# Two layer norms as tensor_scalar, and the router's exponentials as powers of e on GpSimd

## The chip, the cores and the metric

One core of one Trainium2 chip. The metric is the device time of one execution in microseconds. The engines are TensorE (PE in the views, PEld its weight load), VectorE (DVE), ScalarE (ACT), GpSimd (POOL) and SyncE (SP, which issues DMAs). Each engine works through its own queue in order; semaphores tie them together.

## What is computed

An attention block over 8x8 windows and a mixture of experts, on 8 images of 192 channels and 16x16 pixels (2048 tokens of 192 channels).

```python
x = x + attention(_ln_c(x), Wq, Wk, Wv, Wo_w, Wo_b, rel_pos_bias)   # 12 heads, windows of 64 tokens
t = _to_tokens(x)
t = t + ffn(_ln_t(t), Ws, bs, W1, b1, W2, b2)

def ffn(x):
    route_prob = softmax(xt @ Ws + bs)                # 9 experts
    p, routes = max(route_prob), argmax(route_prob)
    h = gelu(xt @ W1 + b1)                            # 192 -> 768
    out = h @ W2 + b2                                 # 768 -> 192
    final = where(routes == 0, common, p * sel + (1 - p) * common)

def _ln_t(v, eps=1e-05):
    return (v - mean(v)) / sqrt(var(v) + eps)         # over the 192 channels; _ln_c is the same with 1e-06
```

The softmax of the router needs, beside the place of the largest logit, only its probability p: one over the sum of the nine exponentials of (logit - largest logit).

## The kernel before

The 2048 tokens are 16 tiles of 128 tokens (a tile is [128, 192], tokens on the partitions). The program has two stages, and every engine has one list of instructions for both.

**Attention stage.** A software pipeline of steps. In step s each engine runs a fixed program of small functions, each on tile s minus its own lag (DVE_PROGRAM, POOL_PROGRAM and so on hold name and lag). The DVE order in a step is: statistics of the first norm (L862, L864), values (L886), transposed weights (L913), residual and statistics of the second norm (L930 to L935), xh (the second norm, L942), normed (the first norm, L856), head_blocks (L874, two instructions, ka and kc), add_bias (L895), normalise (L921, L925), row_max (L903), and in some steps pieces of the routing. POOL's order is: rstd_1 (L556, L558: variance plus eps, then to the power -1/2), softmax_shift (L550, 128x768, subtracts the row maxima), the low half of one piece of a first weight matrix (L579 and L586), rstd_2 (L556, L558), xh_low (L572), the low half of a piece of a second weight matrix (L591), and from step 12 a scatter of a finished tile's rows to DRAM (L597). In step 2 POOL also clears nine blocks of weights (L605).

Both norms read x2 (the tile), mv (mean and variance per token) and rstd (one over the deviation per token), and write a [128, 192] f32 tile: xn for the attention, xhf for the experts. PE transposes xn (L1108), ACT copies it out (L667), and PE makes queries, keys and values from it in the next step. ACT copies the queries (L674); head_blocks waits for that copy, the scores on PE wait for head_blocks, and so on.

**Expert stage.** 39 tiles: 13 tiles through the common expert 0, 23 tiles of tokens sorted by expert, and the last 3 common ones. PE computes hidden(n) (30 matmuls, L1630) and outputs(n-1) (19 matmuls, L1654 and L1659); ACT applies gelu twice to each half of hidden(n) (hp in f16 at L1429, hf in f32 at L1432); DVE subtracts to get the low part (L1543), and both parts are needed before outputs(n). Tiles 0 to 4 overlap with the end of the attention stage. At tile DRAIN = 5 DVE copies the shifted logits lg to ex (L1581) and works out from the counts which expert each of the 23 tiles has: tile_counts (L1485 to L1496) and, behind its low parts and keep_y, tile_experts (L1502 to L1515). ACT takes the exponential of ex (L1447, 128x144 f32) behind its gelus of tile 5. DVE's probabilities (L1473 to L1477) wait for it behind the low parts of tile 6 and give pmax and omp, which the outputs of all later tiles are scaled with.

POOL's list continues, behind the last scatter, with the addresses of the sorted tiles and the scatter of their outputs (L1372 to L1378).

Of the kernel before, what the change touches and what calls it, by code (L numbers as in the profile page):

```python
# [1 line left out]

# [3 lines left out]
F32 = mybir.dt.float32  # L6
# [3 lines left out]
ALU = mybir.AluOpType  # L10
ACT = mybir.ActivationFunctionType
# [3 lines left out]
B, C, IMG = 8, 192, 16  # L15
# [4 lines left out]
NT = B * IMG * IMG // T  # L20
TPI = IMG * IMG // T
CH = 96
NE, FF = 9, 768
# [25 lines left out]
DRAIN = 5  # L49
# [31 lines left out]
def build(nc, x, Wq, Wk, Wv, Wo_w, Wo_b, rpb, rel, Ws, bs, W1, b1, W2, b2, out):  # L81
# [4 lines left out]
    with ExitStack() as whole:  # L86
# [47 lines left out]

        stage_1 = attention(nc, locals())
        stage_2 = experts(nc, locals(), stage_1)
        fused(nc, stage_1, stage_2, whole)

# [44 lines left out]
def attention(nc, g):  # L183
# [17 lines left out]
    with ExitStack() as ctx:  # L201
        def sb(name, shape, dt):
            return ctx.enter_context(nc.sbuf_tensor(name, shape, dt))
# [4 lines left out]
        def sem(name):  # L208
            return g["whole"].enter_context(nc.semaphore(name))
# [3 lines left out]
        xn = sb("xn", [128, C], F32)  # L213
# [9 lines left out]
        xhf = sb("xhf", [128, C], F32)  # L223
# [9 lines left out]
        mv = sb("mv", [128, 2, 2, 2], F32)  # L233
        rstd = sb("rstd", [128, 2, 2], F32)
# [81 lines left out]
        xn_ready = sem("xn_ready")  # L316
# [26 lines left out]
        xh_ready = sem("xh_ready")  # L343
# [159 lines left out]
        def gpsimd_part(pool):  # L503
# [98 lines left out]
            def zero_rows(experts):  # L602

                for e in experts:
                    pool.memset(w1s[LC:128, e, BIAS, :], 0.0).then_inc(w1_zeroed, 1)  # L605
                pool.wait_ge(w1_zeroed, experts[-1] + 1)
# [169 lines left out]
        def vector_part(dve, tile):  # L776
# [75 lines left out]
            def normed(t):  # L852
                dve.wait_ge(rstd1, t + 1)
                if t >= 1:
                    dve.wait_ge(xnT_mm, t)
                dve.scalar_tensor_tensor(out=xn[:, :], in0=x2[:, t, :], scalar=mv[:, 0, t % 2, 0:1],  # L856
                                         in1=rstd[:, 0, t % 2:t % 2 + 1].to_broadcast([128, C]),
                                         op0=ALU.subtract, op1=ALU.mult).then_inc(xn_ready, 1)

            def statistics_1(t):  # L860
                dve.wait_ge(x_kept, t + 1)
# [75 lines left out]
            def xh(t):  # L937
                dve.wait_ge(rstd2, t + 1)
                if t >= 1:
                    dve.wait_ge(xh_hi, t)  # L940
                    dve.wait_ge(xh_lo, t)
                dve.scalar_tensor_tensor(out=xhf[:, :], in0=x2[:, t, :], scalar=mv[:, 1, t % 2, 0:1],  # L942
                                         in1=rstd[:, 1, t % 2:t % 2 + 1].to_broadcast([128, C]),
                                         op0=ALU.subtract, op1=ALU.mult).then_inc(xh_ready, 1)

            def keep_logits(t):
                dve.wait_ge(lg_mm, t + 1)
# [62 lines left out]
            table_low()  # L1010
            one_hots(0)
            normed(0)
            away_from_row(1)
            one_hots(1)
            more_constants()
            statistics_1(1)
            keep_values_1(0)
            head_blocks(0)
            normed(1)
            tails()  # L1020
            for step in range(2, STEPS):
                if step == 2:
                    small_weights()
                stages(step, DVE_PROGRAM, (statistics_1, normed, head_blocks, keep_values_1, add_bias, row_max,
                                           weightsT_1, normalise, residual, xh, keep_logits, choose, slots), None)
                if 0 <= step - DRAIN_STEP < DRAIN:
                    tile(step - DRAIN_STEP)
# [254 lines left out]
def experts(nc, g, front):  # L1282
# [21 lines left out]
    def routed_at(j):  # L1304
        return FIRST + j
# [5 lines left out]
    with ExitStack() as ctx:  # L1311
        def sb(name, shape, dt):
            return ctx.enter_context(nc.sbuf_tensor(name, shape, dt))

        def sem(name):
            return g["whole"].enter_context(nc.semaphore(name))
# [2 lines left out]
        hp = sb("hp", [128, 2, 2, NF, T], F16)  # L1319
        y0 = sb("y0", [128, DRAIN, C], F32)  # L1320
        ex = sb("ex", [128, NT, NE], F32)
        big = sb("big", [128, NE * NR], F32)
        cnt = sb("cnt", [128, 5, NE], F32)
        ejf = sb("ejf", [128, 5, NR], F32)
# [14 lines left out]

        chain = sem("chain")  # L1340
        ex_in = sem("ex_in")
        ex_out = sem("ex_out")
        count_mm = sem("count_mm")
        home_kept = sem("home_kept")
# [21 lines left out]
        out_stored = [sem(f"out_stored{i}") for i in range(OB)]  # L1366

        def gpsimd_part(pool):
            pool.wait_ge(front["rows_zeroed"], 16)
            for j in range(NR):  # L1370
                pool.wait_ge(id_loaded[j % YB], 16 * (j // YB + 1))
                pool.tensor_tensor(home_f[:, 1:2], tid[:, j % YB, 1:2], jint[:, j:j + 1], ALU.mult  # L1372
                                   ).then_inc(home_sums, 1)
                pool.wait_ge(home_sums, j + 1)
                pool.tensor_tensor(home[:, j:j + 1], tid[:, j % YB, 0:1], home_f[:, 1:2], ALU.add).then_inc(home_kept, 1)
                pool.wait_ge(home_kept, j + 1)
                pool.wait_ge(y_kept, routed_at(j) + 1)
                pool.indirect_dma_start(out=ys, out_offset=bass.IndirectOffsetOnAxis(ap=home[:, j:j + 1].bitcast(U32), axis=0),  # L1378
                                        in_=yo[:, j % YB, :], in_offset=None
                                        ).then_inc(y_stored[j % YB], 16)  # L1380
# [41 lines left out]
        def scalar_part(act):  # L1422
            def hidden(n):
                for h in range(2):
                    act.wait_ge(h_mm[h], n + 1)
                    if n >= 2:
                        act.wait_ge(h_lo[h], n - 1)
                        act.wait_ge(y_mm, n - 1)
                    act.activation(hp[:, n % 2, 0, HF * h:HF * h + HF, :],  # L1429
                                   p_h[n % 2][h][:, 0:HF * T].rearrange("p (f t) -> p f t", f=HF), ACT.Gelu,  # L1430
                                   scale=1.0 / SF).then_inc(h_hi[h], 1)
                    act.activation(hf[:, n % 2, h, :], p_h[n % 2][h][:, 0:HF * T], ACT.Gelu, scale=1.0 / SF  # L1432
                                   ).then_inc(h_act[h], 1)

            def keep_image(b):
                act.wait_ge(fin_mm, TPI * (b + 1))
                if b >= OB:
                    act.wait_ge(out_stored[b % OB], 16 * (b // OB))
                act.activation(outc[:, b % OB, :, :], p_f[b % 4][0:CH, :].rearrange("p (k n) -> p k n", k=2), ACT.Copy
                               ).then_inc(fin_kept, 1)  # L1440

            def tile(n):
                if n < N:
                    hidden(n)
                if n == DRAIN:
                    act.wait_ge(ex_in, 1)
                    act.activation(ex[:, :, :], ex[:, :, :], ACT.Exp).then_inc(ex_out, 1)  # L1447
                if n == N:
                    for b in range(B):
                        keep_image(b)  # L1450

            return tile
# [153 lines left out]
        def tensor_part(pe):  # L1606
# [83 lines left out]
            return hidden, outputs, counts, tile  # L1690

        return dict(sync=sync_part, gpsimd=gpsimd_part, scalar=scalar_part, vector=vector_part, tensor=tensor_part)


# [25 lines left out]
```

## Time and profile before

| | |
|---|---|
| median of 3 runs | 314.35 us (312.7 to 315.66) |
| the profiled execution | 313.74 us, of which the span is 312.0 us |
| granted TensorE clock, mean | 0.971 of full speed |
| PE busy | 278.2 us, 89% |
| DVE busy | 247.5 us, 79% |
| ACT busy | 189.2 us, 61% |
| POOL busy | 183.1 us, 59% |
| ACT table loads | 4 of 1.283 us |

Times in the views are microseconds from the span's start unless marked ns. Busy shares are means over stages: the attention stage (to about 160 us), where several engines wait for one another within each step, and the expert stage, where PE runs nearly without a gap from 197 us to 301 us.

### The profile page before, as it was taken

How to read it: one execution, taken by the hardware profiler on the slowest of the kernel's cores; microseconds unless marked ns; L12 is line 12 of the kernel's file. 1: busy time of each engine (PE TensorE's matmuls, PEld its weight loads, DVE VectorE, ACT ScalarE, POOL GpSimd, SP SyncE). 2: the span in 40 equal slices, each digit the busy share in tenths (PEclk: the TensorE clock that was granted, in tenths of full speed). 3: DMA queues.
4: the chain of work that ended last, by engine and by line, in shares of the span. 5: the costliest groups of instructions: out<-in, count | busy, mean ns of one | idle time of the engine just before them, and what ended most of it. 6: DMA issues, size and time to landing. Idle time of an engine off the chain costs nothing.

```text
span 312.0 us, 9835 instructions
## 1 busy us (share of the span) xinstructions
PE 278.2 (89%) x3586; PEld 242.3 (78%) x3586; DVE 247.5 (79%) x540; ACT 189.2 (61%) x410; POOL 183.1 (59%) x262
## 2 busy tenths in 40 slices
PE   4995989899999798889799986899999999999993
PEld 4854657677777676667598886899999999999981
DVE  1847899999999889998945563988998898988463
ACT  1527587777777576877764544955465554554643
POOL 4247787888887769988953533000277676666400
PEclk9999899999999799999859999999999999999999
DMA  5614367524243423333330014112123333232066
GB/s 131 182 27 80 94 213 217 149 72 119 86 129 90 127 71 91 116 95 107 115 103 21 19 53 153 67 32 55 32 61 83 71 70 79 66 78 59 28 204 212
DMA packets 43105, 30.08 MB, mean 96 GB/s; under 512 B 20503, under 2 KB 42122, under 8 KB 43059
## 3 DMA queue, kind: packets, MB, share of 16 engines
q1 hardware_dynamic: 40691, 24.80, 29.4%
q0 software_dynamic: 1872, 4.36, 4.3%
q8 instruction: 29, 0.48, 0.7%
q10 hardware_dynamic: 496, 0.31, 0.5%
q14 instruction: 17, 0.14, 0.2%
HBM read 16.65 MB, written 8.91 MB: 82 GB/s over the span
## 4 chain that ended last, share of the span: by engine, by line
PE 63%; DVE 15%; issue 8%; ACT 6%; POOL 4%; DMA 1%; another core or an unknown queue 1%; DVEq 0%; POOLq 0%; ACTq 0%
PE p_s L1630 10%; PE p_t L1630 10%; PE p_qk L1659 10%; PE p_v L1659 8%; PE p_qk L1122 6%; DVE sc L895 4%; PE p_v L1135 4%; PE p_x L1204 3%; DVE kc L874 2%; PE p_t L1162 2%; PE p_n L1196 2%; PE p_s L1081 1%; ACT q L674 1%; DVE ka L874 1%; DVE on L925 1%
## 5 line engine op out<-in xcount | busy, mean ns | idle before, releaser
L1543 DVE TENSOR_TENSOR hp<-hf,hp 128x384 f16<-128x384 f32 x78 | 42.9, 556 | 26.2 <-ACT hf L1432 24.6
L1378 POOL DMA_INDIRECT routed_outputs<-yo,home x23 | 34.8, 1514 | 34.0 <-DVE yo L1558 32.8
L1429 ACT ACTIVATE hp<-p_t 128x384 f16<-128x384 f32 x38 | 18.7, 493 | 29.9 <-PE p_t L1630 27.0
L1429 ACT ACTIVATE hp<-p_s 128x384 f16<-128x384 f32 x40 | 19.8, 495 | 25.9 <-PE p_s L1630 25.8
L556 POOL TENSOR_SCALAR rstd<-mv 128x1 f32<-128x1 f32 x32 | 8.3, 258 | 39.4 <-DVE mv L864 28.7
L1122 PE MATMUL p_qk<-xnT,wT 96*128 96x128 f32 x192 | 25.4, 283 | 0.0
L1122 PEld LDWEIGHTS p_qk<-xnT,wT 96*128 96x128 f32 x192 | 23.3, 196 | 0.4
L1530 DVE COPY w1d<-w1s 128x3072 f16 x23 | 21.9, 954 | 0.6 <-issue 0.6
L1630 PE MATMUL p_t<-tokT,w1d 128*128 128x128 f16 (+1 forms) x360 | 22.4, 219 | 0.0
L550 POOL TENSOR_TENSOR sc<-sc,mx 128x768 f32<-128x768 f32 x15 | 22.1, 1474 | 0.1
L597 POOL DMA_INDIRECT sorted_tokens<-xhl,slot x16 | 16.9, 1054 | 7.8 <-DVE slot L987 4.7
L591 POOL TENSOR_TENSOR w2s<-w2stage,w2s 128x576 f16<-128x576 f32 x16 | 20.5, 1278 | 1.6 <-ACT w2s L738 1.4
L1630 PEld LDWEIGHTS p_t<-tokT,w1d 128*128 128x128 f16 (+1 forms) x360 | 21.2, 97 | 0.0
L1372 POOL TENSOR_TENSOR home_f<-tid,jint 128x1 int32<-128x1 int32 x23 | 9.3, 405 | 20.1 <-DMA tid<-sorted_tokens 19.4
L1630 PE MATMUL p_s<-xhT,w1s 128*128 128x128 f16 x270 | 18.7, 229 | 2.3 <-issue 2.3
L1630 PE MATMUL p_s<-tokT,w1d 128*128 128x128 f16 (+1 forms) x330 | 20.5, 219 | 0.0
L558 POOL TENSOR_TENSOR rstd<-rstd,minus_half 128x1 f32<-128x1 f32 x32 | 18.3, 571 | 2.7
L1659 PE MATMUL p_v<-w2d,hp 128*128 128x192 f16 x216 | 19.8, 246 | 0.0
L1432 ACT ACTIVATE hf<-p_s 128x384 f32<-128x384 f32 x40 | 19.6, 490 | 0.0
L1630 PEld LDWEIGHTS p_s<-xhT,w1s 128*128 128x128 f16 x270 | 17.4, 103 | 2.7 <-issue 2.7
L1630 PEld LDWEIGHTS p_s<-tokT,w1d 128*128 128x128 f16 (+1 forms) x330 | 19.4, 97 | 0.0
L1162 PE MATMUL p_t<-ident,sc 128*128 128x128 f32 x96 | 18.1, 301 | 1.4 <-ACT sc L690 1.4
(221 smaller groups left out, 780.8 us busy)
## 6 DMA issues: line engine op xcount, KB each, us to landing
w2stage<-in_L_ffn_W_dram SPq DMA_DIRECT2D x18, 288.0 KB, 3.2
w1stage<-in_L_ffn_W_dram SPq DMA_DIRECT2D x18, 192.0 KB
w1stage<-in_L_ffn_W_dram SPq DMA_DIRECT2D x36, 96.0 KB
xin<-in_x_dram SPq DMA_DIRECT2D x8, 192.0 KB, 3.5
routed_outputs<-void SPq DMA_DIRECT2D x1, 1536.0 KB, 7.8
w1d<-routed_outputs SPq DMA_DIRECT2D x8, 192.0 KB, 4.0
out_dram<-w2d SPq DMA_DIRECT2D x8, 192.0 KB, 2.8
sorted_tokens<-void SPq DMA_DIRECT2D x9, 128.0 KB
```

The lines of the kernel that those rows point to most:

```text
L550: pool.tensor_tensor(s, s, mx[:, t % 2, :].unsqueeze(2).to_broadcast([128, NH, L]), ALU.subtract).then_inc(s_sub, 1)
L558: pool.tensor_tensor(r, r, minus_half[:, :], ALU.pow).then_inc(done, 1)
L591: pool.tensor_tensor(w2s[:, e, 1, r, :], w2stage[:, r, :], w2s[:, e, 0, r, :], ALU.subtract).then_inc(w2_lo, 1)
L1122: mm = pe.matmul(p_qk[:, c * T:(c + 1) * T], wT[:, k, c * 128:(c + 1) * 128], xnT[:, t % 2, k, :], start=(k == 0), stop=(k == 1))
L1162: mm = pe.transpose(p_t[h][:, n * T:(n + 1) * T], sc[:, t % SB, pair * 2 * L:(pair + 1) * 2 * L], ident[:, :])
L1378: pool.indirect_dma_start(out=ys, out_offset=bass.IndirectOffsetOnAxis(ap=home[:, j:j + 1].bitcast(U32), axis=0), in_=yo[:, j % YB, :], in ...
L1429: act.activation(hp[:, n % 2, 0, HF * h:HF * h + HF, :], p_h[n % 2][h][:, 0:HF * T].rearrange("p (f t) -> p f t", f=HF), ACT.Gelu, scale=1 ...
L1432: act.activation(hf[:, n % 2, h, :], p_h[n % 2][h][:, 0:HF * T], ACT.Gelu, scale=1.0 / SF).then_inc(h_act[h], 1)
L1530: dve.tensor_copy(w1d[:, j % 2, :, :], w1s[:, e, :, :]).then_inc(w1_copied, 1)
L1543: dve.tensor_tensor(hp[:, n % 2, 1, HF * h:HF * h + HF, :], hf[:, n % 2, h, :].rearrange("p (f t) -> p f t", f=HF), hp[:, n % 2, 0, HF * h ...
L1630: mm = pe.matmul(p_h[n % 2][f // HF][:, (f % HF) * T:(f % HF + 1) * T], w[0:rows, a, f * 128:(f + 1) * 128], xT[0:rows, b, :], start=(m == ...
L1659: mm = pe.matmul(y, hp[:, n % 2, a, f, :], w[:, b, f, :], start=False, stop=(f == NF - 1 and m == 2))
```

## The change

Three edits. (1) Both norms become tensor_scalar with two operands of one value per token, in place of scalar_tensor_tensor with the deviation read as a second tensor (a [128, 1] column repeated 192 times). (2) The exponential leaves ACT's list. (3) POOL gets a [128, 16] tile full of e and, behind its last scatter of the attention stage, one tensor_tensor e ** ex over 128x144 elements.

```diff
             def normed(t):
...
-                dve.scalar_tensor_tensor(out=xn[:, :], in0=x2[:, t, :], scalar=mv[:, 0, t % 2, 0:1],
-                                         in1=rstd[:, 0, t % 2:t % 2 + 1].to_broadcast([128, C]),
-                                         op0=ALU.subtract, op1=ALU.mult).then_inc(xn_ready, 1)
+                dve.tensor_scalar(xn[:, :], x2[:, t, :], mv[:, 0, t % 2, 0:1], rstd[:, 0, t % 2:t % 2 + 1],
+                                  ALU.subtract, ALU.mult).then_inc(xn_ready, 1)
...
             def xh(t):
...
-                dve.scalar_tensor_tensor(out=xhf[:, :], in0=x2[:, t, :], scalar=mv[:, 1, t % 2, 0:1],
-                                         in1=rstd[:, 1, t % 2:t % 2 + 1].to_broadcast([128, C]),
-                                         op0=ALU.subtract, op1=ALU.mult).then_inc(xh_ready, 1)
+                dve.tensor_scalar(xhf[:, :], x2[:, t, :], mv[:, 1, t % 2, 0:1], rstd[:, 1, t % 2:t % 2 + 1],
+                                  ALU.subtract, ALU.mult).then_inc(xh_ready, 1)
...
+        euler = sb("euler", [128, NT], F32)
...
+        euler_ready = sem("euler_ready")
...
         def gpsimd_part(pool):
+            pool.memset(euler[:, :], math.e).then_inc(euler_ready, 1)
+            pool.wait_ge(euler_ready, 1)
+            pool.wait_ge(ex_in, 1)
+            pool.tensor_tensor(ex[:, :, :], euler[:, :].unsqueeze(2).to_broadcast([128, NT, NE]), ex[:, :, :], ALU.pow
+                               ).then_inc(ex_out, 1)
             pool.wait_ge(front["rows_zeroed"], 16)
...
             def tile(n):
                 if n < N:
                     hidden(n)
-                if n == DRAIN:
-                    act.wait_ge(ex_in, 1)
-                    act.activation(ex[:, :, :], ex[:, :, :], ACT.Exp).then_inc(ex_out, 1)
```

ACT's list around the exponential, before (hp and hf are the gelus; the rows ahead of the first table load are tile 5, those behind the second are tile 6):

```order
L1429 ACTIVATE hp<-p_t 128x384
L1432 ACTIVATE hf<-p_t 128x384
L1447 ACT_TABLE_LOAD
L1447 ACTIVATE ex<-ex 128x144
L1429 ACT_TABLE_LOAD
L1429 ACTIVATE hp<-p_s 128x384
L1432 ACTIVATE hf<-p_s 128x384
```

Both table loads go with the exponential; of the four loads of the program the two at L650 and in front of tile 0 stay.

POOL's list behind the attention stage, in the changed kernel (its lines are numbered a few higher than before; the first row ends the scatters of the attention stage, home_f and home are the addresses of the first sorted tile):

```order
L598 DMA sorted_tokens<-xhl,slot 20736x512 x7
L1370 MEMSET euler 128x16
L1373 TENSOR_TENSOR ex<-euler,ex 128x144
L1378 TENSOR_TENSOR home_f<-tid,jint 128x1
L1381 TENSOR_TENSOR home<-tid,home_f 128x1
L1384 DMA routed_outputs<-yo,home 4992x192
```

The second and third row are new; nothing else on POOL has moved.

DVE's list in one step of the attention stage, before (the two norms stand one behind the other, ahead of head_blocks):

```order
L930 SCALAR_TENSOR_TENSOR x<-p_x,x 128x192
L933 BN_STATS stat<-x 128x6
L935 BN_AGGR mv<-stat 128x2
L942 SCALAR_TENSOR_TENSOR xhf<-x,mv,rstd 128x192
L856 SCALAR_TENSOR_TENSOR xn<-x,mv,rstd 128x192
L874 TENSOR_TENSOR ka<-p_qk,mask 128x512
L874 TENSOR_TENSOR kc<-p_qk,mask 64x512
```

In the changed kernel the fourth and fifth row read TENSOR_SCALAR; every row stands where it stood.

## Rows read from the trace of the kernel before

**Rows 1.** Busy time of each engine in three stretches, with instruction counts.

```profile
57.00:106.00 49.00, 43.34 (x541) 33.49 (x541) 46.73 (x101) 36.74 (x82) 39.44 (x52) 1.00 0.37 104
106.00:142.00 36.00, 31.93 (x380) 25.27 (x381) 32.05 (x71) 25.36 (x55) 31.13 (x40) 0.95 0.33 99
197.00:303.00 106.00, 105.48 (x1564) 105.14 (x1564) 89.09 (x165) 58.03 (x134) 49.15 (x69) 1.00 0.28 66
```

**Rows 2.** The chain that ended last, one attention step: start, us, what.

```profile
71.18 0.81 PE p_v L1135 x16
...
73.35 1.41 PE p_qk L1122 x12
...
74.78 0.39 ACT q L674
...
75.21 0.17 DVE xn L856
...
77.18 0.96 DVE sc L895
...
78.31 0.37 DVE on L925
...
79.31 0.81 PE p_v L1135 x16
```

**Rows 3.** Timeline of DVE and POOL in that step: start, us, engine, line.

```profile
73.17 1.47 POOL L550 TENSOR_TENSOR sc<-sc,mx 128x768 f32<-128x768 f32 x1
...
74.07 0.78 DVE L942 SCALAR_TENSOR_TENSOR xhf<-x,mv,rstd 128x192 f32<-128x192 f32 x1
...
74.60 1.03 POOL L579 TENSOR_TENSOR w1s<-w1stage,w1s 128x384 f16<-128x384 f32 x1
74.78 1.06 DVE L856 SCALAR_TENSOR_TENSOR xn<-x,mv,rstd 128x192 f32<-128x192 f32 x1
...
75.76 0.68 DVE L874 TENSOR_TENSOR ka<-p_qk,mask 128x512 f32<-128x512 f32 x1
```

**Rows 4.** Timeline: DVE instructions of other kinds, and POOL's beside them.

```profile
9.71 1.28 DVE L849 TENSOR_SCALAR w2s<-sc 113x2048 f16<-113x2048 f16 x2
11.71 0.42 DVE L856 SCALAR_TENSOR_TENSOR xn<-x,mv,rstd 128x192 f32<-128x192 f32 x1 [0.72 <-POOL rstd L558]
...
24.16 0.65 DVE L798 TENSOR_SCALAR xhl<-kio,minus_row 128x16 int32<-128x16 f32 x1
...
104.22 0.33 DVE L987 CAST slot<-r 128x4 uint32<-128x4 f32 x1
...
9.81 1.21 POOL L556 TENSOR_SCALAR rstd<-mv 128x1 f32<-128x1 f32 x1 [5.46 <-DVE mv L864]
...
20.64 6.20 POOL L605 MEMSET w1s<- 64x768 f16 x9
...
103.25 1.28 POOL L591 TENSOR_TENSOR w2s<-w2stage,w2s 128x576 f16<-128x576 f32 x1
```

**Rows 5.** Timeline of ACT, DVE and POOL between tiles 5 and 6.

```profile
193.02 1.28 ACT L1447 ACT_TABLE_LOAD   x1
...
194.65 1.28 ACT L1429 ACT_TABLE_LOAD   x1
...
190.08 0.96 POOL L597 DMA_INDIRECT sorted_tokens<-xhl,slot  x1 [0.30 <-issue]
...
193.03 0.56 DVE L1543 TENSOR_TENSOR hp<-hf,hp 128x384 f16<-128x384 f32 x1 [3.11 <-ACT hf L1432]
...
196.50 0.23 DVE L1515 TENSOR_SCALAR rtile<-ejf,cnt 1x23 int32<-1x23 f32 x1
196.85 0.56 DVE L1543 TENSOR_TENSOR hp<-hf,hp 128x384 f16<-128x384 f32 x1
...
198.09 0.29 DVE L1473 TENSOR_REDUCE r<-ex 128x16 f32<-128x144 f32 x1
```

**Rows 6.** POOL's groups: all powers, and one addition as small.

```profile
L558 POOL TENSOR_TENSOR rstd<-rstd,minus_half 128x1 f32<-128x1 f32 x32 | 18.3, 571 | 2.7
...
L527 POOL TENSOR_TENSOR mask<-mask 128x4 f32<-128x4 f32 x1 | 0.2, 201 | 0.1
```

More of the change, by code:

```diff
@@ L1 @@
+import math
 from contextlib import ExitStack
```

## The prediction

> **What bounds the kernel now.** I read the busy time by stretch first [rows 1]. From 197 to 303 us PE is busy 105.5 of 106 us. There a saving on DVE, ACT or POOL brings nothing, while a late start of PE at 197 us is passed on in full to the end, since nothing later has a gap to absorb it. From 57 to 106 us it is different: DVE is busy 46.7 of 49 us, PE 43.3, and neither is full. So I read the chain of waits for one step there [rows 2]. It runs from the values (PE, 71.18) to the values of the next step (79.31), 8.13 us, and passes queries on PE, the copy of the queries on ACT (74.78 + 0.39 = 75.17), a piece of xn on DVE, then head_blocks, the bias, the normalisation, and PE again. The timeline [rows 3] shows why xn is in it: ka, the first half of head_blocks, could start when the queries are copied at 75.2, but it starts at 75.76, because xn ahead of it on DVE ends at 75.84 (neighbours overlap a little). That is 0.55 us a step.
>
> The same rows say why xn and xhf are long. The same instruction takes 0.42 us when POOL is idle, at 11.71 [rows 4]. In the step xhf starts at 74.07 and ends at 74.85, 0.2 behind the end of POOL's shift (74.64); xn starts at 74.78 and ends at 75.84, 0.2 behind the end of POOL's weight split (75.63). Both read two tensors from SBUF, as POOL's instructions do, and each waits for the POOL instruction it meets, then needs about 0.2 more (192 elements).
>
> **The norms.** Does tensor_scalar avoid the wait? Three rows say that such single-source DVE instructions meet POOL too [rows 4]. A cast of four elements starts at 104.22 and ends at 104.55, just behind POOL's 103.25 + 1.28 = 104.53. A tensor_scalar of 16 elements with a column operand takes 0.65 us during POOL's nine memsets. And two tensor_scalars that start at 9.71 and end at 10.99 hold up a POOL instruction issued at 9.81 until 11.02. So I cost the new norms as waiting for POOL as before, but shorter behind the wait: no row has this form; the two of 2048 f16 elements take 0.64 each, 0.31 ns an element, which bounds it below, and the norm of before bounds it above with 0.42 alone and 0.2 behind a wait. I take 0.3 alone and 0.1 behind a wait.
>
> The larger effect is the order. At 9.71 the two tensor_scalars ran back to back and POOL, waiting since 9.81, got nothing in between. If xhf and xn do the same, xhf waits for the shift until 74.64, ends near 74.75, and xn follows at once, near 75.0, with POOL's split behind both. Then ka starts at 75.21 with the queries: 0.55 saved in each of the six steps of this pattern (xn at 58.5, 66.7, 74.8, 82.9, 91.0, 100.0): 3.3 us. What is late next is the queries' copy itself, PE's chain. In the three steps where xn alone meets POOL (near 30, 36 and 42 us) it saves the 0.1: 0.3 us. From 106 to 142 us POOL is busy 31.1 of 36 us [rows 1], and from about 115 us the scatter stands in its list as well, so I take 0.4 for all of these steps. Against this stand a wait of the norm near 23 us for one of POOL's memsets (0.7 each, by the row of nine), nearly all under ACT's copies, 0.1, and POOL being held some 0.1 longer in the three steps where it is full, 0.3. Bounds: if xn still waits for the split the steps give 0.1 each, in all 1.0; if all is as above and the late steps give theirs too, 5. I take 3.6 off.
>
> The Trainium skill, SBUF — State Buffer, section "Who interferes with whom", says that tensor_scalar in its two-port mode contends with every GpSimd instruction, also one that only writes, and that whoever issues first has the shared ports for the whole instruction. By that rule POOL's split, issued ahead of xn, would go first, xn would wait for it as today, and the sum would be the one with 1.0 for the norms. The memset row agrees with its first half; the row at 9.71 does not show the second.
>
> **The exponential leaves ACT.** Two table loads of 1.28 and the exponential between them go, 2.9 us of ACT from 193.02 to 195.93 [rows 5]. But tile 6's low part on DVE, for which PE waits, stands behind tile_experts, which ends at 196.50 + 0.23 = 196.73, and it starts at 196.85. So ACT was late by 0.12 us only: 0.1 off. The cover is DVE's own work; without it the edit would be worth up to 2.9.
>
> **The powers on POOL.** POOL's last scatter ends at 190.08 + 0.96 = 191.04; with memset and hand-over the power starts at about 191.25. Call its duration P. No row shows a power of more than one element per partition. That one takes 571 ns, an addition as small 201 [rows 6], so a power costs 370 ns more, either once per instruction or per element. Once: 0.57 + 143 x 1.9 ns (the shift's 1.47 us over 768 elements, rows 3) = 0.84 us. Per element: 0.2 + 144 x 0.37 = 53.5 us. The same row gives both ends; with no other near, I take the middle in ratio, 6.7 us, 44 ns an element. This is a choice, and the weakest in the sum.
>
> Two things wait. DVE's probabilities need the result at 198.09 [rows 5], 6.8 us after the start. But earlier, if a power holds the SBUF ports like POOL's other instructions with two inputs, DVE's low part at 193.03 (two SBUF inputs) waits until it ends, and with it tile_experts, tile 6's low part and PE. So P is free up to 1.8 us, and each us beyond moves the end by one: 6.7 - 1.8 = 4.9 us. The other POOL work behind it (addresses) is not needed before some 210 us.
>
> **Sum.** -3.6 - 0.1 + 4.9 = +1.2 us on the profiled execution's 313.74, so 314.9. That execution lies 0.6 below the median of 314.35, so against the median: 315.5.
>
> **Rivals.**
> Cheap powers (or powers that don't hold DVE and end before 198): P costs nothing, 314.35 - 3.7 = 310.6. For it: 370 ns for one element looks like a fixed part, and a loop over many may fill it. Against: a power is long arithmetic for each element, and POOL's simplest takes 1.9 ns. 0.22.
> Powers at full price per element: P = 53.5, 51.7 late, 362. This is the one on the other side, decided by P: from P = 1.8 + 3.7 + 3.1 = 8.6 us the kernel is slower by over 1%. 0.17. A part of that price, 100 to 200 ns an element, gives P of 15 to 30 and 324 to 339: 0.16.
> xn still waits for the split: norms 1.0 instead of 3.6, with P = 6.7 it gives 318.1. For it: before, POOL got in between the two norms. Against: the pair at 9.71. 0.15.
> My forecast with P between 2 and 14: 0.30, own range 311 to 322.
>
> **Numbers.** The forecast is 315.5. The range starts at 309.5 (cheap powers and a little more from the norms) and reaches 340 (200 ns an element); it leaves out the full price, 0.17. About 1%, 3.1 us, is what a measurement can tell from no change. Faster: the cheap rival and the lowest part of the forecast, 0.23. Within 1%: the forecast with P of 2.4 to 8.6 and the low half of the waiting xn, 0.30. Slower: all else, 0.47.
>
> **What would show it.** In the changed kernel: the power's row on POOL gives P at once. DVE's low part of tile 5 ends 0.4 behind the power if it holds the ports, and takes 0.56 if not. In an attention step xhf ends about 0.1 behind the shift, xn ends before POOL's split has begun, and ka starts with the queries' copy; the values of consecutive steps are then 7.6 us apart, not 8.13. If xn's row still ends behind the split, the pair at 9.71 was the wrong witness. ACT goes from tile 5's gelu to tile 6's without a table load, and DVE's idle time there does not shrink by more than 0.2. What would make the prediction wrong: P outside 2 to 14; the 3.1 us for which DVE waits ahead of 193.03 [rows 5], on an ACT that the trace shows waiting in turn for nothing it names, falling elsewhere, so that tile 5's low part comes earlier and P is covered less; TensorE's clock, which fell in the stretch 106 to 142 (0.95), falling more or less often when the steps are shorter.

## The result, and the profile after

| | before | changed |
|---|---|---|
| median | 315.0 us of 4 (312.7 to 316.15) | 329.86 us of 4 (326.87 to 331.78) |
| ratio to before | | 1.052, 95% interval 1.0465 to 1.0574 |
| the profiled execution | 313.74 us, span 312.0 | 330.84 us, span 329.0 |
| granted TensorE clock, mean | 0.971 | 0.953 |

The changed kernel is 5.2% slower by the recorded ratio. (The recorded ratios are not the quotient of the two medians, and differ from it by up to 0.5%: here the medians alone give 4.7%.) The forecast was 315.5 us in a range from 309.5 to 340. Slower was the likeliest sign and the range holds the time, but the forecast itself was 14.4 us too low, and what happened is the rival with a price of 100 to 200 ns an element, which had a chance of 0.16.

The timeline of the changed kernel from the end of attention on (start, us, engine, line, what, and in brackets the idle time before it and what ended that):

```profile
189.83 23.35 POOL L1373 TENSOR_TENSOR ex<-euler,ex 128x144 f32<-128x144 f32 x1
...
191.32 0.56 DVE L1546 TENSOR_TENSOR hp<-hf,hp 128x384 f16<-128x384 f32 x1 [3.79 <-ACT hf L1438]
...
194.78 0.23 DVE L1518 TENSOR_SCALAR rtile<-ejf,cnt 1x23 int32<-1x23 f32 x1
194.93 1.00 DVE L1546 TENSOR_TENSOR hp<-hf,hp 128x384 f16<-128x384 f32 x2
...
213.22 0.30 DVE L1476 TENSOR_REDUCE r<-ex 128x16 f32<-128x144 f32 x1 [17.28 <-POOL ex L1373]
...
214.26 0.42 DVE L1556 SCALAR_TENSOR_TENSOR x<-p_v,omp,x 128x192 f32<-128x192 f32 x1
...
214.74 0.34 PE L1657 MATMUL p_v<-b2s,ohc 128*128 128x192 f16 x1 [15.85 <-DVE x L1556]
...
215.87 3.06 PE L1662 MATMUL p_v<-w2s,hp 128*128 128x192 f16 x18 [0.79 <-DVE hp L1546]
218.72 2.61 PE L1633 MATMUL p_t<-xhT,w1s 128*128 128x128 f16 x30
...
221.26 1.65 PE L1662 MATMUL p_qk<-w2s,hp 128*128 128x192 f16 x18
222.74 1.86 PE L1633 MATMUL p_s<-xhT,w1s 128*128 128x128 f16 x30
```

The power takes 23.35 us. While it runs DVE goes through its two-input low parts (0.56 us, as in [rows 5]), through tile_experts, and at 194.93 through two more low parts in 1.00 us. Then it comes to the sum over the experts (L1476) and waits 17.28 us. PE, which needs the bank that the scaled outputs (x, L1556) empty, stands for 15.85 us. Behind that gap its first groups are slow: 3.06 us where as many matmuls take 1.65 six us later, and 2.61 where 30 take 1.86. The granted clock shows why (PE alone: busy time, clock, DMA share, GB/s):

```profile
205.00:213.00 8.00, 0.00 (x0) 0.50 0.28 58
...
215.00:218.90 3.90, 3.11 (x21) 0.50 0.00 0
218.90:221.00 2.10, 2.10 (x28) 0.66 0.00 0
221.00:224.00 3.00, 3.00 (x48) 1.00 0.02 5
```

TensorE is at the lower of its two levels (0.50, 1.2 GHz) in the later part of the gap and for some 5 us behind it, and then back at 2.4 GHz.

The busy time by stretch (us of the stretch, then PE, PEld, DVE, ACT, POOL, the granted clock, DMA share, GB/s):

```profile
57.00:106.00 49.00, 44.46 (x549) 34.65 (x548) 46.49 (x104) 37.89 (x83) 39.89 (x55) 1.00 0.37 108
106.00:142.00 36.00, 32.14 (x405) 25.33 (x404) 32.95 (x75) 26.95 (x59) 31.30 (x41) 1.00 0.35 102
142.00:197.00 55.00, 46.00 (x657) 40.06 (x656) 34.22 (x102) 33.33 (x74) 36.29 (x38) 0.97 0.27 87
197.00:303.00 106.00, 89.36 (x1308) 88.68 (x1306) 78.56 (x142) 46.40 (x107) 59.54 (x61) 0.92 0.22 49
```

Against [rows 1] PE has lost 16.1 us of busy time in the last stretch and the mean clock there is 0.92, not 1.00. In the first stretch PE is busy 1.1 us longer, with eight more matmuls. DVE's copy of the logits (ex), which ends the attention stage, stands at 184.31 (185.92 before). How much of that is the norms and how much the clock, one execution can't tell: see the last part of the experiments.

One attention step of the changed kernel, POOL and DVE, which answers to [rows 3]:

```profile
74.87 1.47 POOL L551 TENSOR_TENSOR sc<-sc,mx 128x768 f32<-128x768 f32 x1
76.30 0.93 POOL L580 TENSOR_TENSOR w1s<-w1stage,w1s 128x384 f16<-128x384 f32 x1
...
75.78 0.68 DVE L942 TENSOR_SCALAR xhf<-x,mv,rstd 128x192 f32<-128x192 f32 x1
76.38 0.97 DVE L857 TENSOR_SCALAR xn<-x,mv,rstd 128x192 f32<-128x192 f32 x1
77.27 0.68 DVE L874 TENSOR_TENSOR ka<-p_qk,mask 128x512 f32<-128x512 f32 x1
```

xhf ends at 76.46, 0.12 behind the shift (76.34), as forecast. But xn is not done at once: POOL's split gets in again (76.30 to 77.23), and xn ends 0.12 behind it, at 77.35. The step, from the values on PE at 72.82 to those at 80.75, is 7.93 us, not the 7.6 forecast, and was 8.13.

### The profile page after: what moved, and what is told of

Same layout as the page of the kernel before. It is cut to its first block and busy times, and to the rows that moved or that the text cites. A ratio compares the mean times of both kernels' runs of the same rounds, so it can differ in the third digit from the quotient of the medians.

```text
span 329.0 us, 9835 instructions
## 1 busy us (share of the span) xinstructions
PE 280.1 (85%) x3586; PEld 242.4 (74%) x3586; DVE 245.7 (75%) x540; ACT 186.8 (57%) x407; POOL 205.2 (62%) x264
## 3 DMA queue, kind: packets, MB, share of 16 engines
HBM read 16.65 MB, written 8.91 MB: 78 GB/s over the span
## 5 line engine op out<-in xcount | busy, mean ns | idle before, releaser
L1435 ACT ACTIVATE hp<-p_t 128x384 f16<-128x384 f32 x38 | 18.6, 490 | 49.7 <-PE p_t L1633 46.1
L1121 PE MATMUL p_qk<-xnT,wT 96*128 96x128 f32 x192 | 26.2, 289 | 0.0
L1121 PEld LDWEIGHTS p_qk<-xnT,wT 96*128 96x128 f32 x192 | 24.0, 200 | 0.5 <-issue 0.2
L1373 POOL TENSOR_TENSOR ex<-euler,ex 128x144 f32<-128x144 f32 x1 | 23.4, 23352 | 0.1
L1633 PE MATMUL p_s<-xhT,w1s 128*128 128x128 f16 x270 | 17.5, 219 | 1.6 <-issue 1.6
L1186 PEld LDWEIGHTS p_v<-v,pT 128*64 128x64 f32 x384 | 13.1, 143 | 7.7 <-issue 7.6
L1438 ACT ACTIVATE hf<-p_t 128x384 f32<-128x384 f32 x38 | 18.4, 485 | 0.0
```

The lines of the kernel that those rows point to most:

```text
L1121: mm = pe.matmul(p_qk[:, c * T:(c + 1) * T], wT[:, k, c * 128:(c + 1) * 128], xnT[:, t % 2, k, :], start=(k == 0), stop=(k == 1))
L1373: pool.tensor_tensor(ex[:, :, :], euler[:, :].unsqueeze(2).to_broadcast([128, NT, NE]), ex[:, :, :], ALU.pow).then_inc(ex_out, 1)
L1435: act.activation(hp[:, n % 2, 0, HF * h:HF * h + HF, :], p_h[n % 2][h][:, 0:HF * T].rearrange("p (f t) -> p f t", f=HF), ACT.Gelu, scale=1 ...
L1633: mm = pe.matmul(p_h[n % 2][f // HF][:, (f % HF) * T:(f % HF + 1) * T], w[0:rows, a, f * 128:(f + 1) * 128], xT[0:rows, b, :], start=(m == ...
```

## The experiments

In each comparison the kernel before ran beside it on the same chip. Line numbers differ by a few between kernels.

### One part at a time

**e1, the norms alone.** The two statements of the diff for normed and xh, nothing else.

> Only the two norms are changed; the exponential stays on ACT. Theory (from the trace of the changed kernel): xn still waits for POOL's weight split, both norms are only shorter behind their waits, and a step of the attention stage is 0.2 us shorter (7.93 against 8.13 us). That gives 1 to 2 us over the whole stage: 312.5 to 313.5, if TensorE's clock does not fall at 45 us as it did in that trace. Rival: the norms are worth the 3.6 us of the prediction and the late clock ate it: 311. Second rival: the norms bring on the clock's fall in the stretch 35 to 57 us (granted 0.82) and are worth nothing or less: 314 to 316.

Measured: 312.01 us, ratio 0.9954 (0.9929 to 0.9978), which is 1.4 us less (1.0 by the medians). The copy of the logits stands at 184.61, 1.3 us earlier.

**e2, the power alone.** The rest of the diff.

> Only the exponential moves to POOL; the norms are those of before. Theory: the power takes 23.4 us, DVE waits about 17 us for it, PE starts up again at half its clock, and the kernel is 16 to 18 us slower than before: 331 to 333. Rival, that half the loss comes from the norms: 323.

Measured: 334.0 us, ratio 1.0674 (1.0637 to 1.071). The power again takes 23.35 us and DVE waits 17.25 us for it. So the power, not the norms, makes the changed kernel slower.

**e3, the exponential left out.** The logits stay in ex, and the probabilities are worked out from them without the exponential:

```diff
-                if n == DRAIN:
-                    act.wait_ge(ex_in, 1)
-                    act.activation(ex[:, :, :], ex[:, :, :], ACT.Exp).then_inc(ex_out, 1)
...
-                dve.wait_ge(ex_out, 1)
+                dve.wait_ge(ex_in, 1)
```

> The exponential is left out altogether (the sum of the logits takes the place of the sum of exponentials, so the mixing weights differ); nothing else is changed. It shows what taking two table loads and the exponential off ACT is worth. Theory: tile_experts on DVE covers ACT's 2.9 us, gain 0.1 us, 315. Rival: ACT's backlog behind the loads costs PE too, gain up to 2.9 us, 312.

Measured: 313.02 us, ratio 1.001 (0.9982 to 1.0039). Taking the exponential and its two table loads off ACT, and putting nothing in their place, brings nothing that can be measured. The timeline of this kernel shows DVE's own work still standing there:

```profile
196.37 0.22 DVE L1512 TENSOR_SCALAR rtile<-ejf,cnt 1x23 int32<-1x23 f32 x1
196.52 1.01 DVE L1540 TENSOR_TENSOR hp<-hf,hp 128x384 f16<-128x384 f32 x2
197.11 1.66 PE L1656 MATMUL p_qk<-w2s,hp 128*128 128x192 f16 x18 [0.89 <-DVE hp L1540]
```

The same row in the kernel before:

```profile
197.47 1.68 PE L1659 MATMUL p_qk<-w2s,hp 128*128 128x192 f16 x18 [1.12 <-DVE hp L1543]
```

From the copy of the logits (185.84) to PE's outputs of tile 6 (197.11) it is 11.27 us, and 11.55 before (185.92 to 197.47): 0.3 us, where 0.12 was forecast.

### The price of the power, and what it holds up

**e4, a quarter of the power.** The changed kernel with the power over four of the sixteen tiles; the other tiles keep their logits.

```diff
-            pool.tensor_tensor(ex[:, :, :], euler[:, :].unsqueeze(2).to_broadcast([128, NT, NE]), ex[:, :, :], ALU.pow
+            pool.tensor_tensor(ex[:, 0:4, :], euler[:, 0:4].unsqueeze(2).to_broadcast([128, 4, NE]), ex[:, 0:4, :], ALU.pow
```

> The changed kernel with the power over the first 4 of 16 tiles, 36 elements per partition, in place of 144 (the other tiles keep their logits unexponentiated). Theory, the cost is per element: 0.57 + 35 x 0.159 = 6.1 us, it ends as DVE needs it, and the time is that of the norms alone, 312 to 314. Rival, the 23.35 us are mostly a fixed part (a first call with a wide operand, or the repeated operand): near 20 us and 326 to 330.

Measured: 310.16 us, ratio 0.9907 (0.9873 to 0.9942). From its timeline:

```profile
189.68 6.15 POOL L1373 TENSOR_TENSOR ex<-euler,ex 128x36 f32<-128x36 f32 x1
...
194.77 1.00 DVE L1546 TENSOR_TENSOR hp<-hf,hp 128x384 f16<-128x384 f32 x2
...
195.87 0.30 DVE L1476 TENSOR_REDUCE r<-ex 128x16 f32<-128x144 f32 x1
```

(6.15 - 0.571)/35 = 159 ns for each element beyond the first, and from the whole one (23.35 - 0.571)/143 = 159 ns: a straight line through 1, 36 and 144 elements in a partition. The power ends at 195.83 just as DVE comes to the sum (195.87) and costs nothing: 6.15 us is what is free. From the copy of the logits to the end it is 125.7 us (184.12 to 309.8), and 126.1 in the kernel before. The median is 2 us below the 312 to 314 that was expected; the trace shows nothing behind the copy of the logits that would explain it.

**e11, half of the power**, in the same way over eight tiles. The edit also made another tile, ws16, twice as large as before; no instruction uses the added part.

> The changed kernel with the power over the first eight tiles (72 elements in a partition) alone; the other eight tiles' numbers stay logits, so the weights of the choice are left wrong for them. Theory (159.5 ns per element, free until DVE has come to the sum over the experts): the power takes 0.571 + 71 x 0.1595 = 11.9 us; with a quarter it took 6.15 us, ended as DVE came to the sum (195.83 and 195.87), and the kernel took 310.2 us. So DVE now waits 5.7 us, and the time is 310.2 + 5.7 = 316 us, 315 to 317.5 with the time that PE loses at half clock behind its gap. Rival (the price per element falls with size, or the wait is taken up by work that DVE and PE can do meanwhile): 311 to 314 us.

Measured: 320.19 us, ratio 1.0193 (1.0136 to 1.025); its profiled execution has a span of 316.2.

```profile
187.99 11.89 POOL L1373 TENSOR_TENSOR ex<-euler,ex 128x72 f32<-128x72 f32 x1
...
199.91 0.30 DVE L1476 TENSOR_REDUCE r<-ex 128x16 f32<-128x144 f32 x1 [5.53 <-POOL ex L1373]
201.43 0.32 PE L1657 MATMUL p_v<-b2s,ohc 128*128 128x192 f16 x1 [4.10 <-DVE x L1556]
202.56 3.06 PE L1662 MATMUL p_v<-w2s,hp 128*128 128x192 f16 x18 [0.81 <-DVE hp L1546]
205.42 3.23 PE L1633 MATMUL p_t<-xhT,w1s 128*128 128x128 f16 x30
208.48 0.25 PE L1657 MATMUL p_qk<-b2s,ohc 128*128 128x192 f16 x1
208.57 1.65 PE L1662 MATMUL p_qk<-w2s,hp 128*128 128x192 f16 x18
```

The power's 11.9 us and DVE's wait came as worked out (5.7 expected, 5.53). The time did not: 10 us above the quarter's (by the ratios 2.9%, 9 us) where 4.8 to 7.3 was expected. The two profiled executions show a part of it: from the copy of the logits to the end it is 133.5 us (182.66 to 316.2) against 125.7 (184.12 to 309.8), 7.9 us: 5.5 of wait, and 2.3 for which the slow groups behind the gap account (3.06 for 1.65 and 3.23 for 1.86, 2.8 us together). The us or two beyond that is most likely the quarter's own low median. A power that costs nothing should give the time of the norms alone (312.01, ratio 0.9954), and from there the half is 8.2 us up, or 7.5 by the ratios: what the traces show. The granted clock is still 1.00 in the gap, up to 201.4, then 0.51 to 208.4, and 1.00 again.

### Is it the table load or the place?

**e7, the exponential split.** The changed kernel, but ACT takes the exponentials of tiles 0 to 11 before its first gelu, where no second table load is needed, and the power on POOL takes only the last four tiles.

```diff
+            def early():
+                act.wait_ge(front["oh_ready"], 3)
+                act.activation(ex[:, 0:12, :], lg[:, 0:12, :], ACT.Exp).then_inc(ex_out, 1)
...
+            pool.tensor_tensor(ex[:, 12:16, :], euler[:, 12:16].unsqueeze(2).to_broadcast([128, 4, NE]),
+                               ex[:, 12:16, :], ALU.pow
```

> The norms as changed; ACT takes the exponentials of tiles 0 to 11 (three of the four routing groups) ahead of its first gelu, while its exponential table is still in, and POOL takes only the last four tiles as powers, 36 elements. No table load between the tiles. Theory: the power takes 6.15 us as over a quarter before, ends as DVE needs it, and the time is about 310, below both kernels. Rival: ACT's wait for the third routing group ahead of the first gelu holds up tile 0 and costs 1 us or more: 311 to 313.

Measured: 312.38 us, ratio 0.9965 (0.9924 to 1.0007). The exponential of 108 elements takes 0.28 us on ACT at 157.76, and the power of the last 36 takes 6.15 us on POOL and is covered. The 310 that was expected did not come; the median lies in the rival's range, but the trace does not show the rival's delay: from the copy of the logits to the end it is 125.6 us (182.78 to 308.4), as in e4, and the profiled execution took 310.1. With a power small enough to hide, the whole idea comes out where the norms alone are (0.9954), since there was nothing to win on ACT (e3).

### What xn waits for

**e5, the waits first.** The norms alone; from step 6 on DVE takes xn's semaphore waits ahead of xhf, so that nothing stands between the two.

> Norms only, and from step 6 on the two semaphore waits of xn (for the deviation and for the transposes of the xn before) stand ahead of xhf, so that on DVE nothing stands between the two norms. Theory A: in the changed kernel POOL's weight split got the shared ports between xhf and xn because DVE's queue had waits between them; now they run back to back as the pair at 9.71 did, xn ends before the split, and a step goes from 7.93 to about 7.6 us: 2 to 3 us below the norms alone, 309 to 310. Theory B: whoever has waited longest gets the ports, POOL's split goes first whatever stands in the queue: the same rows as with the norms alone, 312.

Measured: 311.08 us, ratio 0.9942 (0.9902 to 0.9982), as e1. The step is unchanged at 7.93 us:

```profile
73.95 0.59 DVE L946 TENSOR_SCALAR xhf<-x,mv,rstd 128x192 f32<-128x192 f32 x1
74.46 0.97 DVE L857 TENSOR_SCALAR xn<-x,mv,rstd 128x192 f32<-128x192 f32 x1
75.35 0.68 DVE L874 TENSOR_TENSOR ka<-p_qk,mask 128x512 f32<-128x512 f32 x1
...
74.39 0.93 POOL L579 TENSOR_TENSOR w1s<-w1stage,w1s 128x384 f16<-128x384 f32 x1
```

The waits of xn are not what lets POOL in. The split is under way from 74.39, xn's row begins at 74.46, and xn ends 0.1 behind the split.

**e9, POOL's split behind xn.** The norms alone, and in steps 6 to 15 one more wait on POOL:

```diff
                 if k < 2:
                     pool.wait_ge(w1_hi, 2 * e + k + 1)
+                    if 6 <= now[0] < NT:
+                        pool.wait_ge(xn_ready, now[0] + 1)
```

> The two norms alone (no power), and in the steps from 6 on POOL waits with the low part of an expert's first weights (the first split of its step) until DVE has finished that step's xn. In the run with the norms alone xn took 0.97 us in each step and ended 0.1 us behind that split (0.93 us) on POOL, whether xn's waits stood behind xhf or ahead of it. Theory (the split holds xn): xn comes to 0.37 to 0.5 us, the split starts behind it and everything on POOL behind the split 0.5 us later, which the 0.8 us of idle time in POOL's step takes up; the step shrinks by 0.4 to 0.5 us from 7.93 to 7.5, and over some ten steps the end of attention comes 3 to 5 us earlier than with the norms alone: 307 to 309 us against 312. Rival A (the step is set by another chain, through PE): xn becomes short and the step stays 7.9 us: 311 to 312 us. Rival B (POOL is the second bound): the step stays or grows because the low part of the second weights and the shift of the scores come later: 312 to 314 us.

Measured: 311.72 us, ratio 0.9929 (0.9898 to 0.9961); the interval overlaps that of e1.

```profile
73.50 0.37 DVE L860 TENSOR_SCALAR xn<-x,mv,rstd 128x192 f32<-128x192 f32 x1
74.08 0.69 DVE L877 TENSOR_TENSOR ka<-p_qk,mask 128x512 f32<-128x512 f32 x1 [0.21 <-issue]
...
74.01 0.92 POOL L582 TENSOR_TENSOR w1s<-w1stage,w1s 128x384 f16<-128x384 f32 x1 [0.55 <-DVE xn L860]
```

xn takes 0.37 us: the 0.6 us were the wait for the split, and that is shown. ka now starts with the copy of the queries, 4.14 us behind the step's values on PE (69.94), where it was 4.65 before (71.11 to 75.76). But the step fell only to 7.84 us. Behind ka the rows give back 0.2: PE's transposition of the attention's output (L1198) starts at 77.26, 0.26 behind its input; it goes into the bank out of which ACT copies xnT (76.80 + 0.36 = 77.16).

In the steps at 113 and 122 us e9 does not free xn. There xhf starts ahead of POOL's shift, and xn meets the shift instead of the split:

```profile
113.55 1.47 POOL L551 TENSOR_TENSOR sc<-sc,mx 128x768 f32<-128x768 f32 x1
113.73 1.40 DVE L860 TENSOR_SCALAR xn<-x,mv,rstd 128x192 f32<-128x192 f32 x1
```

xn takes 1.40 us there and 1.53 in the next step, against 0.97 in the changed kernel. In the step at 132 us it is 0.37 again. So e9 frees xn in most of its steps, not in all.

**e13, ACT's copy ahead of its second split**, on top of e9:

```diff
-                       ("keep_queries", 1), ("keep_xhT", 7), ("exponentials", 3), ("xh_high", 6), ("split", 0),
-                       ("keep_normedT", 0), ("weightsT_0", 3))
+                       ("keep_queries", 1), ("keep_xhT", 7), ("exponentials", 3), ("xh_high", 6),
+                       ("keep_normedT", 0), ("split", 0), ("weightsT_0", 3))
```

> The norms alone with POOL's split behind xn, as before, and on ACT the copy of the transposed xn ahead of the second split of its step, not behind it. With the split behind xn on POOL the step came to 7.84 us, not 7.6: ka started 0.5 us earlier, with the copy of the queries, but PE's transposition of the attention's output, which goes into the same bank as that of xn, started at 77.26, 0.10 behind the end of ACT's copy out of the bank (77.16) and 0.26 behind its own input (77.00). Theory (ACT's list is the next bound, by that bank): the copy ends some 1.2 us earlier, the transposition follows its input by 0.05 us and the step falls to 7.6 us; over ten steps that is 2 us more, 0.986 to 0.989 of the kernel before. Rival (pT, which now stands behind the split and the copy just as before, or another of ACT's or PE's rows, sets the step): it stays at 7.8 us or more, and the ratio at 0.993.

Measured: 312.93 us, ratio 1.0012 (0.9979 to 1.0045); the ratio of the means over all seventeen executions of the kernel before is 0.999. The step did fall to the 7.6 us of the prediction, and the kernel did not get faster. The timeline shows 7.63 us from xhf to xhf, and the stretches show where it went in this execution:

```profile
74.36 0.87 DVE L945 TENSOR_SCALAR xhf<-x,mv,rstd 128x192 f32<-128x192 f32 x1
75.16 0.37 DVE L860 TENSOR_SCALAR xn<-x,mv,rstd 128x192 f32<-128x192 f32 x1
...
81.99 0.87 DVE L945 TENSOR_SCALAR xhf<-x,mv,rstd 128x192 f32<-128x192 f32 x1
```

```profile
36.00:40.00 4.00, 4.00 (x26) 0.61 0.53 157
...
100.00:105.00 5.00, 3.37 (x31) 0.90 0.27 80
105.00:110.00 5.00, 5.00 (x41) 0.76 0.40 118
```

(The second view gives PE alone: busy time, clock, DMA share, GB/s.) The clock falls at 36 to 40 and at 105 to 110. The step from 98.63 to 108.28 takes 9.65 us, and the same step in e9 8.10 (97.34 to 105.44), at a clock of 1.00. The copy of the logits comes at 185.53, near where it was before the change. Over the twelve executions the mean granted clock is 0.962, against 0.969 in the seventeen of the kernel before beside them; for e9 it was 0.967 against 0.964. So a lower clock is not a matter of this one execution.

### What comes and goes from one execution to the next

In the first traces with the power the sixteen matmuls of the position bias at 15.7 us took 3.46 us (2.58 before), the start was about 1 us late and the clock fell between 32 and 43 us. It looked like a cost of the change.

**e6, tile and memset only.** The kernel before with the tile euler, its semaphore and its memset.

> The kernel before with only the tile of e, its semaphore and its memset on POOL; no power, the exponential on ACT, the norms as before. All three profiled kernels with the power start 0.87 us late at 19 us (16 matmuls of the position bias take 3.46 us instead of 2.58) and have TensorE at its lower clock between 32 and 43 us. Theory: this comes with the new tile or semaphore, and shows here too: the first statistics of the second tile at 19.9 us instead of 19.04, and 1 to 2 us slower than before. Rival: it has to do with the exponential's place in ACT's list, or is chance: the rows are those of before, and so is the time, 313.

Measured: 312.99 us, ratio 0.9984 (0.9946 to 1.0022), with 3.57 us for those matmuls in its profiled execution and a copy of the logits at 188.16. The rows came as in the theory and the time as in the rival, so this run alone settles nothing; its profiled execution was the slowest of its twelve (315.48).

**e10, the changed kernel again**, not altered.

> The changed kernel unaltered, on the same chip and with the same runs of the kernel before as the two beside it. It was 1.052 times the kernel before; the power alone, measured in another call, was 1.0674, and the norms alone 0.9954, so that the norms seem to give 1.5% beside the power and 0.5% without it. If that difference is the chip's and the call's, the ratio here is 1.062 to 1.064 (332 to 333 us); if the norms do give more beside the power, 1.05 to 1.055 (329 to 330 us).

Measured: 330.87 us, ratio 1.0513 (1.0452 to 1.0574). The same stretches as above, of this execution:

```profile
57.00:106.00 49.00, 44.46 (x547) 34.51 (x546) 46.56 (x104) 37.60 (x83) 39.56 (x55) 0.99 0.38 107
106.00:142.00 36.00, 32.39 (x388) 25.67 (x387) 31.78 (x72) 25.65 (x57) 31.48 (x41) 0.96 0.34 100
142.00:197.00 55.00, 47.85 (x652) 42.07 (x651) 34.30 (x102) 33.27 (x74) 36.01 (x38) 0.91 0.26 86
```

The matmuls took 2.23 us, and the clock fell at other places (0.96 and 0.91 where it was 1.00 and 0.97), with the copy of the logits at 184.25 in the end, 0.06 from the first one. The ratio is the one that was expected if the norms give more beside the power.

**e12, the power alone again**, not altered.

> The power alone, unaltered from the run that gave 1.0674 with 3.46 us for the sixteen matmuls of the position bias at 15.7 us and a copy of the logits at 188.09 us. The changed kernel, run twice, gave 3.46 and then 2.23 us for those matmuls with no line of it altered, and 1.052 and 1.051. If the lateness of the start comes and goes with the execution, the power alone comes out lower here: matmuls near 2.6 us, the copy near 186 us, and 1.060 to 1.064, which leaves the norms 0.8 to 1.2%. If the norms do give 1.5% beside the power, the ratio is again 1.065 to 1.07.

Measured: 332.86 us, ratio 1.0626 (1.0555 to 1.0696); the matmuls took 3.09 us, the copy stands at 186.00 (188.09 in e2) and DVE waits 16.98 us for the power. So the lateness of the start and the places of the clock's falls belong to the execution, not to a line of the kernel; the first reading was wrong. In e13, which has no tile of e, the same matmuls took 3.32 us. Why these matmuls differ was not settled.

The place of the copy of the logits in one execution is therefore weak evidence. It moved by 2.1 us between two executions of the power alone. It also stands at 182.28 in e5 and 184.61 in e1, which have the same step of 7.93 us; from 35 to 57 and from 106 to 142 us the clock was 1.00 and 1.00 in e5, and 0.87 and 0.96 in e1.

## Why the prediction came out as it did

**The price of the power: the term that failed.** The prediction had one row of one element and two ends, 0.84 and 53.5 us, and took the middle in ratio, 6.7 us or 44 ns an element. It is 23.35 us, 159 ns an element. It called this the weakest choice in the sum; the range reached to 200 ns an element, and held the time. No row gave that bound, so that the range held is in part luck. The term was 23.35 - 6.7 = 16.65 us too small. The error of the whole sum is 16.0 us (330.9 - 314.9), because what was free was 4.3 us more than forecast, the norms gave 2.2 less, ACT 0.2 more, and 1.6 of slow clock was missing: 16.65 - 4.3 + 2.2 - 0.2 + 1.6 = 16.0.

**What the power holds: failed, in the other direction.** The step "if a power holds the SBUF ports like POOL's other instructions with two inputs, DVE's low part at 193.03 waits until it ends" did not come true. The three low parts that met the power took 0.56, and 1.00 for two. So the power was free up to about 6.1 us, not 1.8. With the forecast's own P of 6.7 only 0.6 us would have been late, and the forecast would have been near 311. The "cheap powers" rival had this half right.

**A term that was missing.** Behind a gap of 15.85 us (4.10 in e11) PE's first groups run at the lower clock (0.50 granted). From the copy of the logits to the end the changed kernel takes 144.7 us (184.31 to 329.0; 144.65 in e10) and the kernel before 126.1 (185.92 to 312.0). Of these 18.6 us, 17.3 are DVE's wait and 0.3 come back from ACT. The 1.6 that are left go to PE's slower restart, whose two slow groups are 2.2 us longer than later ones (3.06 for 1.65, 2.61 for 1.86). The same stretch takes from 125.1 to 126.1 us in the kernels whose DVE waits for no power, so this split is good to about 1 us.

**ACT's table loads: right.** 0.1 was forecast, 0.3 stands in the trace of e3, and its ratio is 1.001. Work of 2.9 us on ACT was worth nothing that can be measured, because DVE's tile_experts stood beside it.

**The norms: the mechanism half right, the size by the rival.** "xhf waits for the shift, ends near 74.75" was right. "xn follows at once" failed: xn still waited for the split, as the rival with 1.0 us had it and as the rule of the Trainium skill's page SBUF — State Buffer, section "Who interferes with whom", that between GpSimd and a DVE instruction in two-port mode whoever issues first has the shared ports for the whole instruction. In e5 POOL's split is issued 0.07 ahead of xn and goes first, and in e9, where it is issued behind it, xn takes 0.37: the traces agree with that rule, though no run shows in which mode xn ran. The pair at 9.71 of [rows 4] was the wrong witness; why POOL got nothing between those two was not looked into. The norms gave 1.4 us alone (e1). That fits 0.2 in each of the six steps (0.1 from xn's shorter rest behind the split, 0.1 from POOL's split, 0.93 for 1.03), 1.2 us, near the 1.0 of the bound and not 3.6. The 1.3 us by which the copy of the logits came earlier do not confirm it: the trace of e1 is 1.1 us late at 58 us (xhf at 58.85, 57.79 before), where its clock had been at 0.87, makes that good by 127, and gains the rest behind it. Beside the power they seem to give 1.1 to 1.6% (1.0674 and 1.0626 against 1.052 and 1.0513), but the intervals of e12 and of the two runs of the changed kernel leave room for the 0.5% of e1. Behind the copy of the logits the four traces are alike (144.7 and 144.65 us with the new norms, 144.2 and 145.0 without), so in these executions the difference lies in the attention stage. Whether it is the norms or the clock stays open.

**Two-input instructions beside the power.** The Trainium skill, SBUF — State Buffer, section "Who interferes with whom", says that a DVE instruction with two SBUF inputs contends with a GpSimd instruction that reads SBUF. For POOL's subtractions the traces agree: they held the xn of before, which reads two tensors (1.06 us at 74.78 against 0.42 at 11.71, [rows 3] and [rows 4]). For the power they don't. The power reads SBUF too, and held none of the two-input instructions that DVE had in the power's first 6 us, the three low parts among them; after that DVE only waited. The measurement decides; how the power takes its inputs was not looked into.

**Could the 0.53 us a step be had?** In rows, yes, in most steps: e9 frees xn and e13 brings the step to 7.63. In time, no: e13 measures 1.0012, and its trace gives the gain back where TensorE's clock falls. The prediction named the clock in its last sentence as something that could go either way, and gave it no number. That e13's median stands where it does because of the clock is argued, from one profiled execution and from the mean clock of the twelve (0.962 against 0.969 before). No run sets the clock by itself, so it is not shown.

**The sum by what was measured.** 313.74 - 1.4 (norms) - 0.3 (ACT) + 17.3 (wait) + 1.6 (half clock) = 330.9; the profiled execution is 330.84. The rival "partial price" would have said 314.35 - 3.7 + (23.35 - 1.8) = 332.2 for this P. It came near because its other errors cancel in part: 4.3 us of cover left out, against 2.0 too much from the norms and ACT and 1.6 of clock left out.

No version tried is clearly better than the norms alone: e9 has the lowest ratio of those that compute everything (0.9929 against 0.9954, intervals that overlap), and none of these shows a gain from the power.

## What to carry to other kernels

Before work is moved to an engine, its price per element there has to be known at the size at which it will run. One element costs 571 ns, of which the line through the four sizes puts 0.41 us on a fixed part and 0.16 on the element, and the row of one element can't tell these apart. A range from 0.84 to 53.5 us is an answer of its own, and its geometric middle is not an estimate. Ask first what the removed work was worth: here ACT's 2.9 us were worth at most 0.3, so no price on POOL above the free 6 us could have paid. And an engine freed within a step of a pipeline hands the bound on: from xn on DVE to ACT's copy, and then, as far as the traces go, to the clock.

## What the runs showed of the hardware

- A power of two tensors on POOL, f32, takes 0.57 us for one element in a partition, 6.15 for 36, 11.89 for 72 and 23.35 for 144: 159 ns an element. ACT's exponential of 144 takes 0.32 us.
- During such a power DVE's subtractions with two SBUF inputs of 384 elements take 0.56 us, as they do in the kernel before (0.56 at 193.03 of [rows 5]). Three of them were seen, all in the power's first 6.1 us.
- The norm of 192 elements as tensor_scalar with two columns takes 0.37 us alone (0.42 as scalar_tensor_tensor) and, like it, waits for a POOL subtraction that was issued first; it then ends 0.12 behind that (0.2 before).
- Behind a gap of 4 us in PE's work 18 matmuls took 3.06 us and the 30 behind them 3.23, for 1.65 and 1.86 later. Behind one of 16 us it was 3.06 and 2.61. The granted clock was 0.50 to 0.51 over the slow groups (0.66 at the end of the last one) and 1.00 behind them.
- The same unaltered program gave 3.46 and 2.23 us for the same sixteen matmuls, and clock falls in different stretches (0.97 and 0.91 from 142 to 197 us), with times of 330.84 and 330.77 us.
